# GpSimd's last gathers: four go out as before, twelve wait for the last tile's up product

## The reference

```python
logits = xt @ W_router + routing_bias
probs = jax.nn.sigmoid(logits)
scores, idx = jax.lax.top_k(probs, TOPK)                 # 2 of 7 experts for each of 1024 tokens
scores = scores / jnp.sum(scores, axis=-1, keepdims=True)
...
hmid = silu(g) * u                                       # gate and up products, 512 wide
combined = jnp.einsum('tei,eih,te->th', hmid, Wd_r, wts) # down product, weighted and summed
return (shared + combined).reshape(B, S, H)
```

## Time and profile before

| | us |
|---|---|
| median of 3 runs | 899.08 (895.98 to 900.73) |
| profiled execution, its own time | 895.73 |
| its span, first to last instruction | 893.9 |
| PE busy | 811.6 (91%) |
| DVE busy | 499.9 (56%) |
| POOL busy | 330.0 (37%) |
| ACT busy | 296.4 (33%) |
| mean granted TensorE clock | 0.969 of full speed |

### The profile page before, as it was taken

The page is one execution under the profiler, slowest core; times in us unless marked ns, Lnnn a source line. Parts: engine busy times, 40 slices in busy tenths (PEclk is TensorE's granted clock), DMA queues, the critical chain, the costliest instruction groups (busy, mean ns, idle before and its releaser), DMA issues.

```text
span 893.9 us, 15831 instructions
## 1 busy us (share of the span) xinstructions
PE 811.6 (91%) x6050; PEld 600.1 (67%) x6051; DVE 499.9 (56%) x1065; ACT 296.4 (33%) x812; POOL 330.0 (37%) x158
## 2 busy tenths in 40 slices
PE   1799999999899998989998999799989999997982
PEld 1555455554567688877866776688868888886861
DVE  6667866669542336524788777854554434332415
ACT  2213323222432245653157665613302121211110
POOL 0000000000534523644006123432769999992050
PEclk8899999999799999999999999999999999999996
DMA  9947655573420040030159000040464563351154
GB/s 343 359 190 295 233 201 225 228 296 111 196 95 1 1 143 1 1 90 35 47 213 384 16 0 1 1 142 1 156 241 169 188 209 121 135 193 47 47 172 158
DMA packets 46696, 127.01 MB, mean 142 GB/s; under 512 B 4000, under 2 KB 8096, under 8 KB 40752
## 3 DMA queue, kind: packets, MB, share of 16 engines
q1 hardware_dynamic: 37744, 106.29, 32.5%
q10 hardware_dynamic: 6336, 11.54, 3.7%
q0 software_dynamic: 2560, 8.39, 2.9%
HBM read 102.05 MB, written 24.15 MB: 141 GB/s over the span
## 4 chain that ended last, share of the span: by engine, by line
PE 74%; DVE 9%; POOL 5%; DMA 5%; issue 3%; ACT 2%; another core or an unknown queue 1%; SPq 0%; POOLq 0%; DVEq 0%
PE scores L489 10%; PE bank L516 9%; PE bank L994 5%; PE bank L996 5%; PE bank L995 5%; DMA nat<-in_ctx_keys 3%; PE bank L719 2%; POOL x_slots L1195 2%; DVE ctxT L1610 2%; PE bank L720 2%; PE bank L651 2%; PE bank L755 2%; PE bank L564 2%; PE bank L566 2%; PE bank L565 2%
## 5 line engine op out<-in xcount | busy, mean ns | idle before, releaser
L1610 DVE STREAM_TRANSPOSE ctxT<-nat 128x1024 f32<-128x1024 f32 (+3 forms) x120 | 120.7, 1067 | 5.6 <-DMA nat<-in_ctx_keys 5.5
L489 PE MATMUL scores<-ctxT,hn 32*64 32x384 f32 (+2 forms) x2048 | 94.0, 513 | 13.4 <-DVE ctxT L1610 13.4
L516 PE MATMUL bank<-nat,probT 128*64 128x512 f32 (+1 forms) x416 | 94.8, 601 | 0.0
L1088 POOL TENSOR_TENSOR wq_lo<-wq_raw,wq_hi 128x1024 fp32r<-128x1024 f32 x4 | 9.3, 2355 | 227.9 <-ACT wq_hi L1286 227.9
L489 PEld LDWEIGHTS scores<-ctxT,hn 32*64 32x64 f32 x2048 | 64.8, 134 | 38.7 <-issue 27.9
L1209 POOL TENSOR_TENSOR ring_lo<-ring_raw,ring_hi 128x2048 fp32r<-128x2048 f32 x18 | 82.9, 4604 | 1.4
L994 PE MATMUL bank<-ring_hi,xg_lo 128*128 x176 | 73.2, 416 | 0.4 <-DVE y L2144 0.4
L996 PE MATMUL bank<-ring_hi,xg_hi 128*128 x176 | 69.4, 394 | 0.0
L995 PE MATMUL bank<-ring_lo,xg_hi 128*128 x176 | 69.0, 392 | 0.0
L1207 POOL TENSOR_TENSOR ring_hi<-ring_raw,cst 128x2048 fp32r<-128x2048 f32 x18 | 64.9, 3603 | 9.8 <-DMA ring_raw<-in_Wexp 9.8
L516 PEld LDWEIGHTS bank<-nat,probT 128*64 128x64 f32 (+1 forms) x416 | 28.0, 138 | 54.1 <-issue 54.0
(11 more groups left out here) (285 smaller groups left out, 1906.9 us busy)
## 6 DMA issues: line engine op xcount, KB each, us to landing
nat<-in_ctx_keys SPq DMA_DIRECT2D x46, 1024.0 KB, 7.4
ring_raw<-in_Wexp SPq DMA_DIRECT2D x21, 1024.0 KB, 9.5
x_slots<-zeros SPq DMA_DIRECT2D x1, 5632.0 KB, 17.2
y_slots<-zeros SPq DMA_DIRECT2D x1, 5632.0 KB, 32.2
hn<-x_slots ACTq DMA_DIRECT2D x22, 256.0 KB, 3.1
y_slots<-hn ACTq DMA_DIRECT2D x22, 256.0 KB, 2.1
w_raw<-in_Wexp SPq DMA_DIRECT2D x3, 1024.0 KB, 5.2
nat<-in_ctx_keys SPq DMA_DIRECT2D x16, 130.0 KB
```

Of the source, the lines that this page charges most:

```text
L489: last = nc.tensor.matmul(scores4[64 * b:64 * b + 64, i, 0:KEYS_IN[i]], q4[rows_i, j, 64 * b:64 * b + 64], ctxT[rows_i, b, j, 0:KEYS_IN[i] ...
L516: last = nc.tensor.matmul(bank[7][64 * b:64 * b + 64, :], probT[0:n, j, 64 * b:64 * b + 64], nat[k % 2][0:n, b, j, :], start=j == 0, stop= ...
L1610: dve.transpose(dst, src).then_inc(columns_ready, 1)
```

## The change

Before the third group's gathers (k == 2), that is behind gather 4 of 16, GpSimd waits until `rup_full` has counted 22, the end of the last tile's up product. Gathers 1 to 4 go out as before.

```diff
             pool.sem_inc(used_stored, 1)
             pool.wait_ge(used_stored, 1)
             for k in range(NT):
+                if k == 2:
+                    pool.wait_ge(rup_full, TILES)
                 for i in range(2):
                     nc.gpsimd.indirect_dma_start(picked[2 * k + i][:], None, y_slots,
                                                  bass.IndirectOffsetOnAxis(slots[:, k, i:i + 1], 0)).then_inc(picked_loaded[picked_part(k)[0]], 16)
```

## The result

The changed kernel took 889.14 us (median of 14 runs, 884.37 to 893.70). The kernel before, timed beside it on the same chip, took 894.00 us (14 runs, 889.92 to 900.73; the three runs shown ahead of the prediction are among them and have the median 899.08). The ratio is 0.9932, with an interval of 0.9907 to 0.9956: 0.7% faster. That holds for the chip of this measurement, which the record doesn't name.

The account below looks back on a forecast made before the run. It took code loads waiting behind the gathers to set the kernel's end. Span 886.3 plus 1.6 for collisions and 0.7 for shared DMA gave 888.6, 5.3 us less; from the median 899.08 that is 893.8, range 889.4 to 901.

Parts of the forecast that it names:

- 5.3 us: Whole kernel: forecast gain, span 888.6 instead of 893.9 us, applied equally to the measured time.
- the reading of the stall as a load of code: Kernel's end: ACT and DVE idle 8.69 and 6.58 us because their instructions load by DMA behind the gathers.
- The base of the sum: Whole kernel: the 5.3 us gain was subtracted from the median 899.08 us, giving 893.8.
- 899.08 - 9.7 = 889.4: Range's lower end: additions starting at 870.0 instead of 879.73, 9.7 us earlier, is the most the change can give.
- The gathers: GpSimd after its wait: gather 5 starts at 865.5, 6.5 us late; the last starts at 879.3, landing at 882.3.
- The additions' start: DVE's final additions: first one starts at 870.0 instead of 879.73 us.
- Collision with additions: Gathers 9 to 16: about five start inside a DVE addition and wait for its end; 1.6 us, bounds 0 and 8.7.
- Shared DMA: 866.8 to 882.3 us: twelve gathers share the DMA engines with output stores; 0.7 us added, bounds 0 and 2.
- A: DVE's product of tile 21: its second code load still takes 6.4 us, product at 871.6, end 888.8; chance 0.14.
- B: DVE's product of tile 21: load held until the gather burst ends, 6.5 us slower, span 900.4; chance 0.15.
- D: Kernel's end: additions shut gathers out in a row, 4 to 8.7 us, span 891 to 895.7; chance 0.10.
- C: Kernel's end: stalls are not the gathers' doing, additions still start at 879.73, span stays 893.9; chance 0.13.

Follow-up runs that it names:

- e3: Kernel before with 64 more wait instructions at the head of PE's list, gathers untouched; ratio 0.9996.
- e4: Kernel before with 128 more wait instructions at the head of PE's list, gathers untouched; ratio 1.0019.
- e9: Kernel before, unchanged, profiled again on another chip; 887.72 us.
- e5: Kernel before with 16 gathers of a quarter of the bytes and additions over a quarter of the columns; 883.2 us.
- e8: Changed kernel with the last twelve gathers released by the last gate product instead of the up product; 889.68 us, ratio to before 1.0012.
- e11: Changed kernel with twelve gathers released by the last gate product, run on the chip of the repeated kernel before; ratio to before 1.0022.
- e18: Changed kernel with eight gathers ahead and eight held for the last up product, on a further chip; 891.62 us.
- e1: Changed kernel with the wait met early (rup_full 20 instead of 22), so all 16 gathers go in a row; 902.08 us beside 893.6 for before.
- e2: Changed kernel with all 16 gathers held for the last up product, none sent ahead; 893.33 us.

## Why the prediction was right or wrong

It said 893.8 us, 5.3 less than before, in a range of 889.4 to 901, and the time was 889.14. Two steps failed: the base from which the 5.3 us were taken, which made the number wrong, and the reading of the stall as a load of code, which didn't.

**The base of the sum.** "Against the median 899.08 the same 5.3 us give 893.8": that median was of three runs, and beside the kernel after before took 894.0. The same step from there is 888.7, 0.4 us under the measured time. The lower end of the range had the same base: 899.08 - 9.7 = 889.4 was to be the most that could be had, and a change with half of that effect came out 0.3 us below it. As a share, the forecast was 0.59% and the measured gain 0.68%. The profiled execution, 895.73, had pointed to a lower base; the prediction named the 3.35 us between them and took the median all the same.

**The gathers.** Forecast: gather 5 at 865.5, 11.56 us behind gather 1; measured 11.49. The last was to start at 879.3, 25.4 us behind gather 1, without charges, and started 25.87 behind.

**The additions' start.** Forecast 870.0, 16.06 us behind gather 1; measured 16.20. Right in size.

**The reason for it.** "What they lack is neither a product nor a buffer; I read it as their code": wrong. They had their code (e3, e4): DVE had executed the wait just ahead of its product at 870.18, and what the product itself waited for was the count of `rup_full`, 11.43 us late. "Only one core runs, so the unknown releaser is none of the program's own work" was the step that led there, and it is wrong too: the releaser was PE's own count, too far behind its matmul for the view to name it. Neither a product nor a buffer was right, but the third possibility, the news of a product, was not thought of. It shares with the reading of code all that the forecast needed (late while gathers go out, in time when four have gone out and the rest wait). That the step of 5.3 us came so near the 4.98 of the tails is luck as far as this reading goes. Neither reading foresaw that another chip would have no lateness at all.

**The charges.** Collision with additions: 1.6 us forecast; three gathers lost (1.27 + 1.14 + 1.06) - 3 x 0.95 = 0.62. Five of gathers 9 to 16 were thought to start inside an addition; four did, and gather 12 did so 0.04 us before the addition's end and lost nothing. DVE paused twice for gathers. Shared DMA: 0.7 us forecast; gather 12 landed 4.8 us after its issue and not 2.1, so 2.7. The sum said that gather 16 decides; it was gather 12 with eight additions behind it. The end of the additions, forecast 883.8 + 2.3 - 853.94 = 32.2 us behind gather 1, came at 881.20 - 848.72 = 32.5. Errors of 1.0 and 2.0 us, of opposite sign, lie in it, the second partly swallowed because gathers 13 to 16 had room behind: luck again, in part.

**The rivals.** A and B need DVE's product late; it came at the end of its matmuls. D was not seen: at most 0.32 us for one gather. C, "the stalls are not the gathers' doing", doesn't hold where it was measured. But a slower case that is none of these is real, and the list did not have it: before without late signals, in which the held gathers alone cost 4.6 us. It was missed because every rival took before's stall as given. "9.7 is the most the change can give" was right as a limit: e9 stands 9.6 us under before in the tail. The change gets half of it, 4.98.

The Trainium skill ("SBUF — State Buffer", Who interferes with whom) has the first to come block the other for its whole instruction. The charged gathers agree: gather 9 started inside the addition that ended at 864.92 + 0.74 = 865.66 and ended at 865.21 + 1.27 = 866.48, 0.82 us behind it; gathers 10 and 13 ended 0.82 us behind theirs, and scatters 13 and 16 had ended 0.83 us behind the end of their L2151. Each waited for the end of the instruction that it had run into. The Trainium skill ("Runtime: NRT & Kernel Launch", Instruction fetch mechanics) calls the cost of fetching code mostly hidden. The prediction set that aside with "the second does not here", but these traces agree with it: e9 has PE's packet in its tail and no delay, and e4 has the delay and no packet.

**Open.** Whether lateness belongs to a chip or to a time: no chip was knowingly visited twice. Whether every timed run there had it: the medians of before lie 894.0 - 887.7 = 6.3 us apart, and the two profiled tails 9.6. Which property of the gathers brings it: bytes, number or an unbroken run of some 8 us; e5 to e8 and e11 to e18 all fell where nothing is late. Of before and after, before is the faster where signals are in time (887.7 against 892.1), after where they aren't (889.1 against 894.0). The release at the gate product costs 0.1 to 0.3% in the one case (two of the four intervals take in no change) and never ran in the other.

## What to carry to other kernels

An idle time that ends with a "remote" releaser on a single core, with its input long computed, is not proof of a code load: compare the time of the count on its semaphore with the end of the work that makes it, and look whether a transfer of code lies in the gap. Take the kernel before again on another chip before explaining a stall that only traces of one chip show; here the same program had a tail of 40.0 and of 30.3 us, and the change's sign went with it. Forecast a ratio from the profiled execution, and don't carry it to a median of three runs.

## What the runs showed of the hardware

- In the first measurement and on the chip of e1 to e4, while a burst of GpSimd's indirect DMAs ran (256 KB every 1.25 us), PE's counts on semaphores came up to 11.4 us late in before and 11.6 in e3 (DVE's product in before: idle 15.03 us where e9 has 3.61), the last of them 0.8 us after the burst's traffic ended. Signals from DVE to PE were in time while PE's were late (0.46 us idle at 648.94). On the chips of e5 to e18 there was no such lateness, in e9 at 225 GB/s of the same traffic.
- A burst of four gathers, then a pause of 6.7 us and twelve more, had no late signal that anyone waited for, on the chip where 16 in a row had: ACT's copies at 862.70 and 868.19 came 2.5 and 8.0 us behind gather 5 and were in time.
- With the DMA engines full (share 1.01 from 870 to 876 us of the kernel after) gather 12 landed 4.8 us after its issue; the last gather of before, with nothing beside it, took 2.1 us.
- In e2 PE ran tile 21's down product, from 868.30 us on, at a granted clock of 0.50 (1.2 GHz) where the stretch from 864 to 868 us had 1.00: its matmuls came 0.43 us apart instead of 0.23. In those four us PE had been busy for 1.95. ACT's last copy came 1.6 us later for it, off the path.
